# Four probability buffers, LayerNorm rows moved to VectorE, and a new order of all engine queues in a gated attention and mixture-of-experts kernel

## The reference, cut to what matters

```python
# block 0: decayed running sum of ctx*ctx, gated by LayerNorm(x)
r_t = 0.9 * r_(t-1) + ctx_t * ctx_t
x1  = x + tanh(g_xattn[0]) * layernorm(x) * r
# adapter feed-forward on B = layernorm(x1): base product, a projection that
# picks one of four low-rank adapters (ranks 1, 2, 4, 8) and weighs it
x2  = x1 + tanh(g_ffn[0]) * (B @ W.T + gate * (B @ down.T) @ up.T)
# block 1: 16-head attention with sigmoid weights; queries from C = layernorm(x2),
# keys and values from ctx, masked values
x3  = x2 + tanh(g_xattn[1]) * (sigmoid(q @ k.T / 4) @ v) @ Wo
# 8 experts, top 2 per token, on E = layernorm(x3)
out = x3 + tanh(g_ffn[1]) * sum_top2 p_e * (gelu(E @ w_in[e] + b_in[e]) @ w_out[e] + b_out[e])
```

## Time and profile before

| what | value |
|---|---|
| median of 3 runs | 486.82 us (485.8 to 487.15) |
| span of the profiled execution, first to last instruction | 478.9 us |
| median of the runs minus that span | 7.9 us |
| granted TensorE clock, mean over the span | 0.961 |
| PE busy | 396.5 us (83%) |
| PEld busy | 309.2 us (65%) |
| DVE busy | 370.2 us (77%) |
| ACT busy | 330.9 us (69%) |
| POOL busy | 251.4 us (53%) |

### The profile page before, as it was taken

The page is one execution under the profiler, slowest core; times in us unless marked ns, Lnnn a source line. Parts: engine busy times, 40 slices in busy tenths (PEclk is TensorE's granted clock), DMA queues, the critical chain, the costliest instruction groups (busy, mean ns, idle before and its releaser), DMA issues.

```text
span 478.9 us, 13099 instructions
## 1 busy us (share of the span) xinstructions
PE 396.5 (83%) x4092; PEld 309.2 (65%) x4092; DVE 370.2 (77%) x1416; ACT 330.9 (69%) x671; POOL 251.4 (53%) x313
## 2 busy tenths in 40 slices
PE   2758899998999989998899887789568898989950
PEld 1446667776776777676677765478457797777740
DVE  2788888998988889898888785368556566789993
ACT  2755788898889889998888775576616564655640
POOL 1621212545553464637453556678876676766760
PEclk9988999999999999999999999889969999999995
DMA  7336686664575555876454665525353559397975
GB/s 231 90 111 178 181 215 177 183 194 133 166 227 182 162 174 161 244 178 209 144 170 125 220 189 146 166 67 151 90 157 103 165 162 335 101 351 244 330 262 201
DMA packets 69501, 87.12 MB, mean 182 GB/s; under 512 B 9485, under 2 KB 55290, under 8 KB 69306
## 3 DMA queue, kind: packets, MB, share of 16 engines
q1 hardware_dynamic: 60074, 65.81, 47.4%
q0 software_dynamic: 6816, 18.65, 10.5%
q10 hardware_dynamic: 2544, 1.81, 1.2%
HBM read 51.07 MB, written 35.18 MB: 180 GB/s over the span
## 4 chain that ended last, share of the span: by engine, by line
PE 46%; DVE 14%; issue 13%; POOL 11%; ACT 8%; DMA 6%; another core or an unknown queue 1%; ACTq 1%; DVEq 0%; POOLq 0%; SPq 0%
PE ps_J L1654 13%; PE ps_F L1654 6%; PE ps_O L1768 5%; PE ps_T L1663 5%; PE ps_S L1755 4%; POOL store_x L765 4%; POOL pause_t L782 3%; PE ps_S L1654 3%; DMA store_y<-y_out,y_row 2%; POOL store_y L771 2%; PE ps_R L1693 2%; DVE y_out L2938 2%; PE ps_O L1779 2%; PE ps_G L1654 2%; DMA temp_t<-in_temp 2%
## 5 line engine op out<-in xcount | busy, mean ns | idle before, releaser
L771 POOL DMA_INDIRECT store_y<-y_out,y_row x78 | 78.4, 1005 | 41.6 <-DVE y_out L2938 29.5
L765 POOL DMA_INDIRECT store_x<-xn_E,slot_u x64 | 68.8, 1076 | 27.1 <-DVE slot_u L2637 16.9
L1093 ACT ACTIVATE prob<-ps_S 128x512 f32<-128x512 f32 x128 | 72.4, 594 | 12.0 <-PE ps_S L1755 7.6
L1755 PE MATMUL ps_S<-q_stack,k_stack 128*128 128x256 f16 x256 | 44.5, 276 | 5.6 <-issue 3.5
L2926 DVE TENSOR_TENSOR h_lo<-h_f,h_hi 128x512 f16<-128x512 f32 x39 | 26.9, 689 | 24.5 <-ACT h_hi L1177 19.6
L1654 PE MATMUL ps_J<-wout_hi,h_hi 128*128 x112 | 31.2, 278 | 15.2 <-DVE y_out L2938 12.9
L1768 PE MATMUL ps_O<-prob,v_wide 128*32 128x128 f32 x1024 | 41.0, 279 | 1.1 <-ACT prob L1093 0.9
L1169 ACT ACTIVATE h_f<-ps_F,bin_t 128x256 f32<-128x256 f32 x56 | 23.5, 471 | 25.9 <-PE ps_F L1654 20.1
L1654 PE MATMUL ps_F<-xb_hi,win_hi 128*128 128x256 f16 x112 | 31.8, 284 | 4.1 <-DVE xb_lo L2907 2.7
L1779 PE MATMUL ps_O<-wo_t,av 128*128 128x256 f32 x128 | 32.8, 401 | 2.3 <-ACT av L1121 1.6
L751 POOL TENSOR_TENSOR rstd_C<-var_C,minus_half 128x2 f32<-128x2 f32 x16 | 12.2, 761 | 40.3 <-DVE var_C L2416 40.3
(11 more groups left out here) (302 smaller groups left out, 1410.6 us busy)
## 6 DMA issues: line engine op xcount, KB each, us to landing
parts_scratch<-parts SPq DMA_DIRECT2D x32, 256.0 KB
k_stack<-parts_scratch SPq DMA_DIRECT2D x64, 128.0 KB
q_stack<-parts_scratch SPq DMA_DIRECT2D x128, 64.0 KB
xb<-store_x SPq DMA_DIRECT2D x30, 257.0 KB
y_got<-store_y SPq DMA_DIRECT2D x14, 512.0 KB
c_in<-in_ctx SPq DMA_DIRECT2D x16, 256.0 KB
x_in<-in_x SPq DMA_DIRECT2D x16, 256.0 KB
store_x<-zeros SPq DMA_DIRECT2D x15, 257.0 KB, 4.8
```

The costliest lines, as they stand in the source:

```text
L765: pool.indirect_dma_start(store_x, bass.IndirectOffsetOnAxis(slot_u[q][:, at:at + 1], 0), xn_e[q][:, at, :], None).then_inc(s_scat[q], 16)
L771: pool.indirect_dma_start(store_y, bass.IndirectOffsetOnAxis(y_row[n][:, b:b + 1], 0), y_out[n][:, b, :], None).then_inc(s_y_kept[n], 16)
L1093: act.activation(prob[m % PROBS][:, 2 * n:2 * n + 2, :, :], bank_s[n], ACT.Sigmoid, scale=float(HD) ** -0.5).then_inc(s_prob[n], 1)
L1755: ins = pe.matmul(bank_s[n][:, g % 2, :, :], k_stack[q][:, g, k, cut], q_stack[q][:, :, g, k, cut], start=True, stop=True)
```

## The change

Four things change.

1. `PROBS` is 4. Buffers 0 and 1 stay, and 2 and 3 lie where `w_f32`, the fp32 weights of the setup, lay. `sigmoids(0, 2, n)` therefore waits until the four low parts of the weights are made. Some other buffers lie elsewhere, and `add_bias(4)` waits for the last `weigh`.
2. x1 is made without a shift: `moves` computes (x - mean) * running sum in two VectorE instructions of 128x256, and `make_x1` computes moved * gain + x in two more. `gained` and `shifts_a` are gone.
3. `normed_b` and `normed_c` run on VectorE, two `tensor_scalar` of 128x256 each with mean and reciprocal deviation as per-partition scalars. Their shifts are gone.
4. All queues are in another order. The tiles are written out as well. TensorE transposes some blocks two ahead. GpSimd's pauses keep their numbers, 39 and 32, and stand elsewhere. The setup starts with other transfers and with `squared(0)` ahead of `gates_tanh`.

```diff
-PROBS = 2
+PROBS = 4
-        prob = [sb(f"prob{i}", [128, 4, 2, 128]) for i in range(PROBS)]
+        prob = [sb(f"prob{i}", [128, 4, 2, 128]) for i in range(2)]
+        setup = ExitStack()
+        w_f32 = setup.enter_context(nc.sbuf_tensor("w_f32", [128, KT, WCOLS], F32, side="right"))
+        setup.close()
+        prob += [right(f"prob{i}", [128, 4, 2, 128]) for i in range(2, PROBS)]
...
             def sigmoids(p, m, n):
                 act.wait_ge(s_score[n], 4 * p + m + 1)
                 need(act, s_pv, 4 * p + m + 1 - PROBS)
+                if p == 0 and m == 2:
+                    act.wait_ge(s_wlo, 4)
...
-            def gained(p):
-                q = p % 2
-                act.wait_ge(s_shift["A"], p + 1)
-                need(act, s_x2, p - 1)
-                for b in range(2):
-                    act.activation(x1[q][:, b, :], x_in[q][:, b, :], ACT.Identity, bias=shift["A"][q][:, b:b + 1],
-                                   scale=ln_gain[q][:, b:b + 1]).then_inc(s_xn["A"], 1)
...
             def moves(p):
+                q = p % 2
                 dve.wait_ge(s_scan, p + 1)
-                dve.wait_ge(s_xn["A"], 2 * p + 2)
-                need(dve, s_x1, p)
-                dve.tensor_tensor(moved[:, :, :], x1[p % 2][:, :, :], bank_r, ALU.mult).then_inc(s_moved, 1)
+                dve.wait_ge(s_aggr["A"], 2 * p + 2)
+                need(dve, s_x1, 2 * p)
+                for b in range(2):
+                    dve.scalar_tensor_tensor(out=moved[:, b, :], in0=x_in[q][:, b, :], scalar=mv["A"][q][:, b, 0:1],
+                                             in1=bank_r[:, b, :], op0=ALU.subtract, op1=ALU.mult).then_inc(s_moved, 1)
             def make_x1(p):
                 q = p % 2
-                dve.wait_ge(s_moved, p + 1)
-                dve.tensor_tensor(x1[q][:, :, :], moved[:, :, :], x_in[q][:, :, :], ALU.add).then_inc(s_x1, 1)
+                dve.wait_ge(s_moved, 2 * p + 2)
+                dve.wait_ge(s_gain, p + 1)
+                need(dve, s_x2, p - 1)
+                for b in range(2):
+                    dve.scalar_tensor_tensor(out=x1[q][:, b, :], in0=moved[:, b, :], scalar=ln_gain[q][:, b:b + 1],
+                                             in1=x_in[q][:, b, :], op0=ALU.mult, op1=ALU.add).then_inc(s_x1, 1)
+            def normed(k, p, src):
+                dve.wait_ge(s_rstd[k], p + 1)
+                need(dve, s_t[k], p)
+                for b in range(2):
+                    dve.tensor_scalar(xn[k][:, b, :], src(b), mv[k][p % 2][:, b, 0:1], rstd[k][p % 2][:, b:b + 1],
+                                      ALU.subtract, ALU.mult).then_inc(s_xn[k], 1)
```

The order of GpSimd around the change from pairs to tiles, before and after (cut):

```diff
             inverse_root("E", 15)
             keep_block(0, 0)
-            long_pause()
             keep_block(0, 1)
-            long_pause()
+            scatter(14, 3)
+            scatter(14, 2)
             keep_block(1, 0)
             long_pause()
+            long_pause()
             keep_block(1, 1)
-            long_pause()
             keep_block(2, 0)
-            long_pause()
             keep_block(2, 1)
-            long_pause()
-            scatter(15, 3)
-            long_pause()
...
+            scatter(14, 1)
+            scatter(14, 0)
             keep_block(3, 0)
-            long_pause()
             keep_block(3, 1)
+            keep_block(4, 0)
+            keep_block(4, 1)
+            keep_block(5, 0)
+            keep_block(5, 1)
+            keep_block(6, 0)
+            scatter(15, 3)
+            scatter(15, 0)
+            scatter(15, 1)
+            keep_block(6, 1)
+            scatter(15, 2)
+            keep_block(7, 0)
```

More of the change, by code:

```diff
@@ L981, in _ @@
[L981 to L996 removed]
+            pause()
+            keep_block(13, 1)
+            keep_block(14, 0)
@@ new lines, in _ @@
+            keep_block(21, 0)
+            keep_block(21, 1)
+            keep_block(22, 0)
+            keep_block(22, 1)
+            keep_block(23, 0)
+            keep_block(23, 1)
+            pause()
+            pause()
+            pause()
+            pause()
+            pause()
+            pause()
+            pause()
+            pause()
+            keep_block(24, 0)
+            keep_block(24, 1)
+            keep_block(25, 0)
+            keep_block(25, 1)
+            pause()
+            pause()
@@ L3822, in _ @@
             adapter_gated(15)
-            next(early)
             down_hi(15)
@@ L3985, in _ @@
-            for n in range(TILES + 1 - ADD_AT, NP):
-                add_pair(n)
+            add_bias(9)
+            hidden_lo(10)
+            take_rows(10)
+            copy_lo(12)
+            add_bias(10)
+            router_diff(15)
+            hidden_lo(11)
+            take_rows(11)
+            copy_lo(13)
+            add_bias(11)
+            take_rows(12)
+            hidden_lo(12)
+            next(final)
+            copy_lo(14)
+            take_rows(13)
+            add_bias(12)
@@ new lines, in _ @@
+            hidden_lo(13)
+            copy_lo(15)
+            add_bias(13)
+            hidden_lo(14)
+            copy_lo(16)
+            take_rows(14)
+            take_rows(15)
+            copy_lo(17)
+            add_bias(14)
+            hidden_lo(15)
+            hidden_lo(16)
+            add_bias(15)
+            copy_lo(18)
+            take_rows(16)
+            take_rows(17)
+            add_bias(16)
+            copy_lo(19)
+            hidden_lo(17)
+            next(gates)
+            take_rows(18)
@@ new lines, in _ @@
+            next(gates)
+            hidden_lo(18)
+            next(gates)
+            copy_lo(20)
+            copy_lo(21)
+            add_bias(17)
+            hidden_lo(19)
+            take_rows(19)
+            add_bias(18)
+            copy_lo(22)
+            hidden_lo(20)
+            hidden_lo(21)
+            copy_lo(23)
+            add_bias(19)
+            take_rows(20)
+            add_bias(20)
+            copy_lo(24)
+            hidden_lo(22)
+            take_rows(21)
+            add_bias(21)
@@ new lines, in _ @@
+            hidden_lo(23)
+            take_rows(22)
+            add_bias(22)
+            take_rows(23)
+            copy_lo(25)
+            hidden_lo(24)
+            copy_lo(26)
+            next(gates)
+            add_bias(23)
+            hidden_lo(25)
+            take_rows(24)
+            take_rows(25)
+            take_rows(26)
+            next(gates)
+            next(gates)
+            copy_lo(27)
+            take_rows(27)
+            add_bias(24)
+            hidden_lo(26)
+            next(gates)
@@ new lines, in _ @@
+            next(gates)
+            copy_lo(28)
+            take_rows(28)
+            add_bias(25)
+            add_bias(26)
+            hidden_lo(27)
+            add_pair(0)
+            copy_lo(29)
+            add_pair(1)
+            hidden_lo(28)
+            add_bias(27)
+            copy_lo(30)
+            hidden_lo(29)
+            copy_lo(31)
+            add_bias(28)
+            add_pair(2)
+            add_pair(3)
+            hidden_lo(30)
+            take_rows(29)
+            copy_lo(32)
```

2283 lines of the change are left out of this document (1312 added, 971 removed).

## The result

The changed kernel takes 495.37 us (median of 4 runs, 492.24 to 499.83) where the kernel before takes 486.31 (4 runs, 483.74 to 487.15). The ratio is 1.0177 with a 95% interval of 1.0126 to 1.0228, so it is slower by 1.8%. Forecast were 471.3 us and faster. The profiled execution took 492.24 us with a span of 490.3.

A forecast was written before the change was run, and what follows sets the result against it. It saw TensorE (94%) and VectorE (89%) nearly full in the pairs, with idle time at the setup and the transition. Terms 0 - 3 - 8 - 3 - 1.5 = -15.5 us took 486.8 to 471.3 us, own range 466 to 475.

The forecast's parts named there:

- the transition's -8: From pairs to tiles: fewer GpSimd pauses partly remove the 7.5 us hole and low clock; -8 us (-12 to -2).
- the last tiles' -1.5: Last tiles: one pair's adds, 1.6 us, move into VectorE's 4.88 us tail wait; -1.5 us (-2 to 0).
- Rows on VectorE: Pair stage: added VectorE instructions less removed products and shifts cost +1.4 us a pair (+0.9 to +1.8).
- the pair stage: Run of pairs: shorter hand-overs, new order and buffers pay for the dearer VectorE; 0 us (-6 to +9).
- The buffers' part: Pair stage: probability buffers help pay for VectorE but alone give little; ScalarE waited 2.3 us for `weigh`.
- Setup: Before the pairs: with `squared(0)` first the running sum starts up to 3 us earlier; -3 us, bounds 0 and -6.
- a steady 0.2 us a pair for GpSimd's interference: Pair stage: GpSimd may slow the four new `tensor_scalar`, +0.2 us per pair, kept for the range.
- each pause taken from between two transfers frees 0.65 us of GpSimd: Transition, GpSimd's queue: a transfer with a pause costs 1.99 us, without one 1.34, so 0.65 us is freed.
- Tiles 8 to 26: Tile stage: transposing two ahead shortens a tile from 3.52 to 3.35 us; -3 us (-6 to +1).
- a result buffer has five pairs of time: Last tiles: late stores on SP stand behind later loads, but each result buffer has five pairs of time.
- Tail: Behind the last `y_out`: the chain is unchanged, its distance to the end still 14 to 15 us.
- Slower through VectorE's queue: Rival, pair stage: dearer `tensor_scalar` and GpSimd interference make a pair 18.0 us, 489 us in all; chance 0.13.

The follow-up runs named there:

- after_again: The changed kernel itself, unchanged, run again on a chip without late tellings: 460.93 us against 467.99, ratio 0.988.
- before_again: The kernel before, unchanged, profiled again on a chip without late tellings: 469.12 us, one run.
- b3_struct: The changed functions and four probability buffers, all in the order of the kernel before: 481.42 us, ratio 1.0303.
- b2_short: The kernel before with the 18 long GpSimd pauses of the transition made short, nothing else changed: 462.64 us, ratio 0.9859.
- a7: The changed kernel up to the first tile, then the order of the kernel before with short pauses in the transition: 462.5 us, ratio 0.9892.
- a2: The changed kernel with all engines but GpSimd back in the old order from tile 15 on: 493.72 us, ratio 1.0115.
- a5: The changed kernel with long GpSimd pauses in the transition, short ones from tile 7, and the other engines' old order from tile 15: 471.68 us, ratio 1.0038.
- a10: The changed kernel with all engines in the order of the kernel before from tile 24 on: 459.02 us, ratio 0.9814.
- a11: The changed kernel with the old order from tile 11 on, GpSimd with one short pause a tile from tile 8: 464.42 us, ratio 0.9887.
- a12: The changed kernel with all engines in the old order from tile 15 on: 456.35 us, ratio 0.9728.
- a4: The changed kernel with long GpSimd pauses between the transition's indirect DMAs and one short pause a tile from tile 7: 481.06 us, ratio 1.0275.
- a1: The changed kernel with short GpSimd pauses put back between its indirect DMAs, other engines as changed: 503.14 us, ratio 1.0271.
- a3: The changed kernel with short GpSimd pauses put back and the other engines' old order from tile 15 on: 491.62 us, ratio 1.0093.

## Why the prediction was wrong

The profiles without late tellings show what each term of the sum was worth; the profile of the result shows what became of it. Two steps failed above all: the transition's -8, which became +4.2 behind late tellings, and the last tiles' -1.5, which became +6.7 with or without them.

**Rows on VectorE.** The `scalar_tensor_tensor` was right: two take 0.86 to 0.88 us. The `tensor_scalar` was mis-sized at 0.29. VectorE's groups and a stretch of its timeline in the changed kernel:

```profile
L2807 DVE TENSOR_SCALAR xn_B<-x,mv_B,rstd_B 128x256 f32<-128x256 f32 x32 | 14.2, 485 | 0.3 <-POOL rstd_B L815 0.3
L2791 DVE SCALAR_TENSOR_TENSOR moved<-x_in,mv_A,ps_R 128x256 f32<-128x256 f32 x32 | 13.9, 474 | 1.9 <-PE ps_R L1883 1.9
L2807 DVE TENSOR_SCALAR xn_C<-xs,mv_C,rstd_C 128x256 f32<-128x256 f32 x32 | 12.4, 430 | 0.5 <-POOL rstd_C L815 0.3
```

```profile
201.69 0.86 DVE L2807 TENSOR_SCALAR xn_C<-xs,mv_C,rstd_C 128x256 f32<-128x256 f32 x2
202.47 0.73 DVE L2755 BATCH_NORM_STATS2 stats_E<-xs 128x6 f32<-128x256 f32 x2
```

Two take 202.47 - 201.69 = 0.78 us, 0.39 each, so my sum per pair becomes +1.8 us, the upper bound. That the order pays for it was right and by more than I granted. Without late tellings a pair took (304.7 - 67.8) / 15 = 15.8 us in after_again, between 15.7 and 16.4 in the ten kernels that share this pair half, and 16.4 in before_again. In the profile of the result it is 16.39 for 16.67. I took 0 us for the pair stage. It is -9 in after_again and -4 in the result's profile, where four late tellings of 7.3 us stand on the chain. The buffers' part was nothing in the old order, as the earlier trace rows said.

**Setup.** Forecast -3, measured +1.8 (first `make_x3` at 67.4 us for 65.6). The running sum did move, from 10.44 to 7.06 us:

```profile
7.06 2.05 PE L1883 MATMUL ps_R<-kv,decay_t 128*128 128x512 f32 x2 [7.06 <-ACT kv L1191]
...
19.70 1.11 PE L1853 MATMUL ps_T<-ident,xn_B 128*128 128x128 f32 x4 [2.68 <-DVE xn_B L2807]
```

But what pair 0 waited for next was its normed rows, and those met GpSimd's two memsets. VectorE and GpSimd:

```profile
16.64 3.00 DVE L2807 TENSOR_SCALAR xn_B<-x,mv_B,rstd_B 128x256 f32<-128x256 f32 x2
19.56 0.86 DVE L2791 SCALAR_TENSOR_TENSOR moved<-x_in,mv_A,ps_R 128x256 f32<-128x256 f32 x2
```

```profile
16.49 1.79 POOL L849 MEMSET q_stack<- 128x2048 f32 x1
18.23 0.94 POOL L852 MEMSET v_wide<- 128x1024 f32 x1
19.15 0.72 POOL L846 TENSOR_TENSOR pause_t<-half_ones,minus_half 128x2 f32<-128x2 f32 x1
```

Two `tensor_scalar` take 3.00 us instead of 0.86: the first takes 2.68 and ends at 19.32, just after the second memset (19.17). In b3_struct the same one takes 3.64 us. The Trainium skill, SBUF — State Buffer, Who interferes with whom, says that a `tensor_scalar` in a two-port mode and GpSimd shut each other out for whole instructions; these rows agree with it for memsets, by 2.1 us. They don't bear it out for GpSimd's other work: all the others of the 64 in this profile stay between 0.39 and 0.60, although 55 of them lie beside something on GpSimd. The longest five of these, 0.53 to 0.59 us, lie beside an indirect DMA.

The memsets are not all of the 4.8 us between forecast and measurement. The variance of pair 0 was ready at 13.87 us, but its deviation stood behind another instruction in GpSimd's queue:

```profile
13.68 2.19 POOL L856 TENSOR_TENSOR sim_inv<-sim_sq,minus_half 64x4 f32<-64x4 f32 x1 [1.67 <-DVE sim_sq L3349]
15.85 0.69 POOL L815 TENSOR_TENSOR rstd_B<-var_B,minus_half 128x2 f32<-128x2 f32 x1
```

So the deviation started at 15.85 us, where the kernel before had it at 15.50, and the 3.4 us gained at the running sum were gone before the memsets came. My estimate had a steady 0.2 us a pair for GpSimd's interference, and I had not looked at what GpSimd does at the one moment when TensorE has nothing else.

**From pairs to tiles.** Forecast -8 (-12 to -2). Without late tellings tiles 0 to 8 take 27.5 us for 39.3: -11.8, and b2_short shows that shorter pauses alone give 6.0 of it in the old order. The mechanism was right. Windows of before_again (312 to 354) and after_again (305 to 336), from about 3 us ahead of the `y_out` of tile 0 to that of tile 8:

```profile
312.00:354.00 42.00, 30.35 (x269) 25.84 (x269) 29.00 (x89) 23.44 (x44) 36.54 (x41) 0.92 0.42 124
```

```profile
305.00:336.00 31.00, 29.11 (x269) 24.40 (x268) 26.83 (x79) 20.57 (x42) 24.41 (x26) 1.00 0.50 157
```

The same 269 matmul rows take 31 us at a granted clock of 1.00, where they took 42 us at 0.92. In the result's profile the stage takes 44.4 us for 40.3: +4.2 (the ends rounded) in place of -8. The late tellings at 332 and 353 us, 5.6 and 6.6 us on the chain, and one of 2.9 at 323 are 15.1 us together, close to the 16.0 between +4.2 and -11.8. **This is the step that failed most:** "each pause taken from between two transfers frees 0.65 us of GpSimd" holds, but on the chip of the result the freed queue goes with waits of 3 to 7 us. The trace of before has eight such waits in its tile half, none above 2.6 us, and my sum had no term for them.

**Tiles 8 to 26** were forecast at -3. They take +3.8 (67.2 for 63.4), with 9.1 us of late tellings on the chain for 4.3, and +2.8 without any (60.2 for 57.4). So the new order gains nothing here. 2.4 of the 2.8 us lie in tiles 8 to 15, where the splice with the old order (a7) is back at 22.6 us. What in the order costs them is not shown.

**Last tiles.** Forecast -1.5, measured +6.7, and +6.3 without late tellings. This term was wrong on every chip, and a2, a5, a7, a10, a11 and a12, which put the old order back there, take 4 to 6 us of it away. One reading of the cause, from VectorE's timeline in after_again:

```profile
415.17 0.68 DVE L3288 TENSOR_TENSOR h_lo<-h_f,h_hi 128x512 f16<-128x512 f32 x1
419.04 0.88 DVE L3318 SCALAR_TENSOR_TENSOR result<-y_got,gate_all,xs 128x256 f32<-128x256 f32 x2 [3.20 <-DMA out<-result]
419.84 0.88 DVE L3325 SCALAR_TENSOR_TENSOR result<-y_got,gate_all,result 128x256 f32<-128x256 f32 x2
420.63 0.68 DVE L3302 TENSOR_TENSOR y_out<-ps_S,bout_t 128x512 f32<-128x512 f32 x1
```

An add waits for its result buffer, whose store stands late in SP's queue, and two `y_out` stand behind it in VectorE's. The prediction named exactly this and let it go with "a result buffer has five pairs of time". Only whole orders were exchanged, so how much of the 6.3 us is SP's and how much the bursts of two tiles is argued, not shown.

**Tail.** 14.2 us for 14.7, as forecast. Behind the last `y_out` stand five pairs' adds, not the four that the signs at the end of the prediction name.

Without late tellings the terms add up: 2.4 - 9.3 + 1.0 (last `make_x3` to tile 0) - 11.8 + 2.8 + 6.3 + 0.6 = -8.0 us, and the spans differ by 466.7 - 458.6 = 8.1. In the result's profile they give 1.8 - 4.2 - 0.4 + 4.2 + 3.8 + 6.7 - 0.5 = +11.4, the difference of its spans. Even without late tellings the forecast of -15.5 would have missed: the pair stage and the transition gave more than forecast, and the setup, tiles 8 to 26 and the last tiles cost 5.4, 5.8 and 7.8 us more. None of my rivals was this one. "Slower through VectorE's queue" had the sign and not the mechanism. No wait for `xb<-store_x` is above 1.8 us in any profile; the hole that came back with long pauses (a4) is the old one, at `y_row`. Of the signs named beforehand the pace of `project` ((312.8 - 64.0) / 15 = 16.6 us), the running sum at 7.06 us and the missing wait of `y_row` came. What did not come is TensorE above 80% busy at a clock near 1 over tiles 0 to 8: it is busy 29.65 of 44.40 us (67%) at 0.91.

**What stays open.** What a late telling is. The pair half of the changed kernel narrows it. In the kernel before a scatter there starts 0.95 us or more behind the end of the one before, and there is no `remote` wait. In the changed kernel groups of four scatters with 0.30 us between them stand there four times. GpSimd's rows of the third group (the first and the last of the four), and then ScalarE's `parts` behind it, whose product is complete on TensorE's rows at 220.43 us:

```profile
217.28 1.04 POOL L829 DMA_INDIRECT store_x<-xn_E,slot_u  x1 [0.18 <-issue]
...
221.16 0.96 POOL L829 DMA_INDIRECT store_x<-xn_E,slot_u  x1 [0.30 <-issue]
```

```profile
223.03 0.60 ACT L1225 ACTIVATE parts<-ps_J 128x512 f16<-128x512 f32 x1 [2.21 <-remote]
```

The four such groups end at 152.4, 170.7, 222.1 and 275.8 us, and within 1.1 us of each end a late telling of 1.7 to 2.2 us ends on the chain:

```profile
151.58 1.74 another core or an unknown queue
169.80 1.66 another core or an unknown queue
220.82 2.19 another core or an unknown queue
275.04 1.73 another core or an unknown queue
```

The profiles of a1, a2 and a3, which share this code and the chip of the first four, show a `remote` wait at such a group in 11 of 12 cases, and mostly at the same instruction: this same `parts` waits 2.26, 2.23 and 2.10 us. Every `remote` wait in these four pair halves ends at most 1.1 us behind the end of a group of two or four. So late tellings are no accident of one execution; they belong to places in the program where GpSimd issues several indirect DMAs without a pause. That is not all of it. The two groups of three in that half have none, only one of the groups of two has one (to 251.2 us), after_again has the same groups and no late telling at all, and short pauses did not remove them in the tile half: with one and the same GpSimd queue they are 3.7 us on the chain of a1 over tiles 0 to 8 and 15.6 in a3. The test that takes the indirect stores away ran twice, both times on a chip that has no late tellings. So it is not proved by an edit that GpSimd causes them, whether TensorE finishes late or is told late is open, and so is what sets the chips apart: the median durations of single instructions agree within 4% on both, but for GpSimd's short pauses.

## What to carry to other kernels

A change that fills queues more tightly can change its sign from chip to chip (1.8% slower and 1.2% faster here): compare a gain of one or two per cent on more than one chip, and look for waits that no row explains before crediting or blaming an order. Cost an order stage by stage and keep, per stage, the better one: here the changed transition (27.5 us for 39.3) and the old last tiles (40.7 for 47.0) belong together, and the kernel with both (a12) is 2.7% faster than the one before on a chip without late tellings. How it does on one with them is not known. Before adding what lies around a span to it, compare with other executions of which both numbers are known. A step moved onto VectorE has to be looked up against GpSimd's memsets at the moment when another engine waits for it.

## What the runs showed of the hardware

- The kernel before takes 486 to 488 us on one or two chips and 468 to 469 on four others, with the median durations of TensorE's, VectorE's and ScalarE's instructions the same within 4%. 4 us of the 12 between the spans of before and before_again lie in the pair half and 7 in tiles 0 to 26. Late tellings on the chain are 4.3 us of the 12.
- On the dearer chip a product that is complete on TensorE's rows can reach idle engines 3 to 6 us later, in bunches (360.22 and 361.78 above), and it does so behind groups of unpaused indirect DMAs on GpSimd: at 15 of the 16 groups of four in the pair halves of four profiles.
- A `tensor_scalar` of 128x256 takes 0.41 us in the median, and one that met two memsets on GpSimd 2.68.
- The same code up to the first tile ended between 302.6 and 312.7 us on chips without late tellings: ten us that no edit made. Stage times of a single profile are to be read with that in mind.
